# VectorE exponentials split with bitwise operations, and 512 more columns of channel 14 moved to VectorE in units 16 to 31

## What is computed

```python
def wl_step(acc, wl):
    cpm, iw = wl
    m = cpm[None, :, None, None]
    Qw = Q * m
    Kw = K * m
    scores = jnp.einsum('bhqd,bhkd->bhqk', Qw, Kw) * SCALE
    scores = scores * jnp.cos(KERR * scores * scores)
    attn = jax.nn.softmax(scores, axis=-1)
    out = jnp.einsum('bhqk,bhkd->bhqd', attn, V)
    return (acc + out * iw, None)
acc, _ = jax.lax.scan(wl_step, acc0, (cos_pm, interference_weights))
combined = acc / WL_CHANNELS
```

## Time and profile before

| | us |
|---|---|
| median of 3 runs | 3400.6 (3398.81 to 3402.12) |
| the profiled execution, its own time | 3405.69 |
| span of its trace | 3403.6 |
| ScalarE busy | 3316.2 (97%) |
| VectorE busy | 3240.6 (95%) |
| TensorE matmuls busy | 2650.6 (78%) |

### The profile page before, as it was taken

The page is one execution under the profiler, slowest core; times in us unless marked ns, Lnnn a source line. Parts: engine busy times, 40 slices in busy tenths (PEclk is TensorE's granted clock), DMA queues, the critical chain, the costliest instruction groups (busy, mean ns, idle before and its releaser), DMA issues.

```text
span 3403.6 us, 47606 instructions
## 1 busy us (share of the span) xinstructions
PE 2650.6 (78%) x20639; PEld 760.4 (22%) x20639; DVE 3240.6 (95%) x2747; ACT 3316.2 (97%) x611; POOL 229.2 (7%) x321
## 2 busy tenths in 40 slices
PE   7777877777777777778778788888877778788876
PEld 2212222222222222222222222222222222222224
DVE  7999999999999999999999999999999999999997
ACT  7999999999999999999999999999999999999992
POOL 0000000000000000000001111101111101111100
PEclk8999899999999999998999999899999999988888
DMA  1000000000000000000000000000000000000001
GB/s 49 1 1 1 1 1 1 1 1 1 1 1 1 1 1 1 1 15 1 1 1 3 4 3 4 2 1 4 2 4 2 4 1 2 4 3 16 2 17 31
DMA packets 21400, 16.05 MB, mean 5 GB/s; under 512 B 4865, under 2 KB 19602, under 8 KB 20946
## 3 DMA queue, kind: packets, MB, share of 16 engines
q1 hardware_dynamic: 19922, 12.28, 1.2%
q10 hardware_dynamic: 1152, 0.53, 0.1%
q0 software_dynamic: 128, 0.26, 0.0%
HBM read 7.70 MB, written 5.37 MB: 4 GB/s over the span
## 4 chain that ended last, share of the span: by engine, by line
ACT 59%; issue 32%; ACTq 4%; DVE 2%; PE 2%; DMA 0%; POOL 0%; DVEq 0%
ACT probs L694 56%; ACTq L684 4%; ACT probs L691 3%; PE psum L1392 1%; ACTq L688 0%; DVE s_t L921 0%; DVE probs L973 0%; DVE m_pad L909 0%; DMA iw<-nterference_weights_dram 0%; PE psum L948 0%; DVE probs L1003 0%; PE psum L1063 0%; PE psum L943 0%; PE psum L1106 0%; PE psum L933 0%
## 5 line engine op out<-in xcount | busy, mean ns | idle before, releaser
L694 ACT ACTIVATE probs<-s_t 128x8192 f32<-128x8192 f32 x447 | 3099.8, 7054 | 2.8 <-PE psum L1392 2.8
L1392 PE MATMUL psum<-probs,v_pad 128*27 128x512 f32 x15136 | 1909.2, 646 | 638.0 <-ACT probs L694 605.5
L1392 PEld LDWEIGHTS psum<-probs,v_pad 128*27 128x27 f32 x15136 | 462.1, 113 | 1996.9 <-issue 1022.1
L765 DVE SCALAR_TENSOR_TENSOR x_y<-s_t,c_last,x_2k 128x2048 f32<-128x2048 f32 (+1 forms) x160 | 369.6, 2310 | 2.3
L777 DVE SCALAR_TENSOR_TENSOR x_p<-x_p,x_y 128x2048 f32<-128x2048 f32 (+1 forms) x160 | 358.3, 2239 | 4.5
L785 DVE SCALAR_TENSOR_TENSOR x_p<-x_p,x_2k 128x2048 f32<-128x2048 f32 (+1 forms) x160 | 357.7, 2236 | 3.9
L781 DVE SCALAR_TENSOR_TENSOR x_p<-x_p 128x2048 f32<-128x2048 f32 (+1 forms) x160 | 357.3, 2233 | 2.4
L773 DVE SCALAR_TENSOR_TENSOR x_p<-x_y 128x2048 f32<-128x2048 f32 (+1 forms) x160 | 356.8, 2230 | 0.0
L921 DVE COPY s_t<-psum 128x2048 f32<-128x2048 f32 x128 | 292.2, 2284 | 9.4 <-PE psum L884 9.0
L909 DVE TENSOR_REDUCE m_pad<-psum 128x4 f32<-128x2048 f32 x128 | 292.4, 2286 | 5.8 <-PE psum L844 4.6
L762 DVE TENSOR_SCALAR x_2k<-s_t,c_last 128x2048 int16<-128x2048 f32 (+1 forms) x160 | 201.2, 1257 | 4.9 <-issue 1.0
(11 more groups left out here) (245 smaller groups left out, 1083.9 us busy)
## 6 DMA issues: line engine op xcount, KB each, us to landing
s_t<-in_L_attn_x_dram SPq DMA_DIRECT2D x4, 256.0 KB, 7.3
x_next_dram<-x_p SPq DMA_DIRECT2D x1, 1024.0 KB, 4.0
x_group<-x_next_dram SPq DMA_DIRECT2D x1, 1024.0 KB, 4.8
loop_memory<-in_L_attn_x_dram SPq DMA_DIRECT2D x8, 128.0 KB, 2.3
x_dram<-loop_memory SPq DMA_DIRECT2D x8, 128.0 KB, 1.8
out_dram<-loop_memory SPq DMA_DIRECT2D x8, 128.0 KB, 1.8
x_dram<-probs SPq DMA_DIRECT2D x2, 512.0 KB, 4.8
out_dram<-probs SPq DMA_DIRECT2D x2, 512.0 KB, 3.6
```

Of the source, the lines that this page charges most:

```text
L694: nc.scalar.activation(probs[:, (p + w) % 2, :], s_t[:, p, :], ACT.Exp, scale=scales[(p + w) % 2]).then_inc(s["exp_done"], 1)
L765: nc.vector.scalar_tensor_tensor(out=y, in0=scores, scalar=scale, in1=at, op0=ALU.mult, op1=ALU.subtract) \
L1392: last = nc.tensor.matmul(products_of(u, wg)[L * b:L * b + SLOTS * A, :], v_pad[:, p, b * T + kt, c0:c0 + SLOTS * A], probs[:, (p + w) % 2 ...
```

## The change

The split of a piece into integer and fraction is done in another way. Op 0 now writes an int32 fixed-point number with 23 fraction bits (the scale has a factor 2^23). Op 1 is a `tensor_scalar` of two bitwise operations that cuts the fraction bits out and sets the exponent of 1.0, in place of a `scalar_tensor_tensor` that read scores and integer. Op 2 is a `tensor_scalar` of two bitwise operations on int32 in place of arithmetic on int16. Ops 3 to 6 keep their form with other constants; op 6 reads an f32 power of two in place of a bf16 one. The work tile grows from 2 to 4 bytes an element, and `one_row` moves from a tile of its own, filled by GpSimd at the start, to a place in `s_t`, filled by VectorE in the last unit.

`SHARED_B` becomes (4, 4): in both groups ScalarE does 6144 columns of channel 14, and the fifth piece has all 2048 columns of its last key tile. In group 0 that is as before; in group 1 (units 16 to 31) 512 columns go from ScalarE to VectorE, and two matmul records from L1392 to L798. The tables for a sixth piece are written but `SHARED_B` leaves them unused: `pieces_of` is 5 for every unit, and the steps are those of before.

```diff
-SHARED_B = (0, 1)
-ACT_LAST = [T * X_COLS - (NB - b) * S for b in SHARED_B]
-PIECES = T + 1
+SHARED_B = (4, 4)
+ACT_LAST = [(T - 1) * X_COLS - (NB - b) * S for b in SHARED_B]
+def pieces_of(u):
+    return T + 1 + (SHARED_B[u // H] < NB)
+def piece_no(u, n):
+    return sum(pieces_of(v) for v in range(u)) + n
...
-        x_2k = sb("x_2k", [P, X_COLS], BF16)
-        x_n = x_2k[:].bitcast(I16)
+        x_i = sb("x_i", [P, X_COLS], I32)
...
-            w, start, cols = (W - 1, n * X_COLS, X_COLS) if n < T else (WA - 1, ACT_LAST[u // H], T * X_COLS - ACT_LAST[u // H])
+            w, start, cols = ((W - 1, n * X_COLS, X_COLS) if n < T else (WA - 1, (T - 1) * X_COLS, X_COLS) if n == T
+                              else (WA - 1, ACT_LAST[u // H], (T - 1) * X_COLS - ACT_LAST[u // H]))
...
-            at, y, t = x_n[:, 0:cols], x_y[:, 0:cols], x_p[:, piece % 2, 0:cols]
+            at, y, t = x_i[:, 0:cols], x_y[:, 0:cols], x_p[:, piece % 2, 0:cols]
             if op == 0:
                 dve.wait_ge(s["piece_ready"], piece + 1)
                 nc.vector.tensor_scalar(at, scores, scale, LOWEST_Y, ALU.mult, ALU.max).then_inc(s["piece_chain"], 1)
             if op == 1:
                 dve.wait_ge(s["piece_chain"], base + 1)
-                nc.vector.scalar_tensor_tensor(out=y, in0=scores, scalar=scale, in1=at, op0=ALU.mult, op1=ALU.subtract) \
+                nc.vector.tensor_scalar(y.bitcast(I32), at, FRACTION_BITS, ONE_BITS, ALU.bitwise_and, ALU.bitwise_or) \
                     .then_inc(s["piece_chain"], 1)
             if op == 2:
                 dve.wait_ge(s["piece_chain"], base + 2)
-                nc.vector.tensor_scalar(at, at, 127.0, 128.0, ALU.add, ALU.mult)
+                nc.vector.tensor_scalar(at, at, EXPONENT_TOP, EXPONENT_BITS, ALU.bitwise_xor, ALU.bitwise_and)
...
-                nc.vector.scalar_tensor_tensor(out=t, in0=t, scalar=EXP2_D, in1=x_2k[:, 0:cols], op0=ALU.add, op1=ALU.mult) \
+                nc.vector.scalar_tensor_tensor(out=t, in0=t, scalar=EXP2_D, in1=at.bitcast(F32), op0=ALU.add, op1=ALU.mult) \
                     .then_inc(s["piece_ready"], 1)
...
-                            for b in range(SHARED_B[g] if w == WA - 1 and kt == T - 1 else NB):
+                            for b in range(NB if w < WA - 1 or kt < T - 2 else SHARED_B[g] if kt == T - 2 else 0):
```

More of the change, by code:

```diff
@@ L73, in steps_of @@
 def steps_of(u, usual, last):
-    return last if u == UNITS - 1 else usual
+    return last if u == UNITS - 1 else usual[u // H]
 def due(u, w, usual, last):
@@ L218, in postln_kernel @@
         gate_b = scratch(G + EXPERTS)
+        one_row = scratch(P)
         assert taken[0] <= T * NB * S
@@ L227, in postln_kernel @@
         order = sb("order", [P, EXPERTS])
-        one_row = sb("one_row", [P, P])
         index = sb("index", [P, 3, MT], I32)
@@ L511, in _ @@
             nc.gpsimd.memset(quarter[:], 0.25)
-            nc.gpsimd.memset(one_row[:], 1.0)
             nc.gpsimd.memset(w_head[:], 0.0).then_inc(s["masks_zeroed"], 1)
@@ L784, in piece_dve @@
                 dve.wait_ge(s["piece_chain"], base + 5)
-                nc.vector.scalar_tensor_tensor(out=t, in0=t, scalar=EXP2_D, in1=x_2k[:, 0:cols], op0=ALU.add, op1=ALU.mult) \
+                nc.vector.scalar_tensor_tensor(out=t, in0=t, scalar=EXP2_D, in1=at.bitcast(F32), op0=ALU.add, op1=ALU.mult) \
                     .then_inc(s["piece_ready"], 1)
         def piece_pe(pe, n, u):
-            pe.wait_ge(s["piece_ready"], u * PIECES + (n + 2))
+            pe.wait_ge(s["piece_ready"], piece_no(u, n) + 2)
             if n == 0:
                 pe.wait_ge(s["o_copied"], max(u * NWG + 1, 2))
-            wg, kt = (NWG - 1, n) if n < T else (LAST_OF[WA - 1], T - 1)
+            wg, kt = (NWG - 1, n) if n < T else (LAST_OF[WA - 1], T - 1 if n == T else T - 2)
             c0 = VPAD if n < T else VPAD - A * SLOT_OF[WA - 1]
-            for b in range(NB) if n < T else range(SHARED_B[u // H], NB):
-                at = b * S if n < T else (b - SHARED_B[u // H]) * S
+            first, latest = SHARED_B[u // H] if n > T else 0, pieces_of(u) - 1
+            for b in range(first, NB):
+                at = (b - first) * S
                 last = nc.tensor.matmul(products_of(u, wg)[L * b:L * b + SLOTS * A, :],
-                                        v_pad[:, u % 2, b * T + kt, c0:c0 + SLOTS * A],
-                                        x_p[:, (u * PIECES + n) % 2, at:at + S], start=(n == 0), stop=(n == T - 1 or (n == T and u < UNITS - 1)))
+                                        v_pad[:, u % 2, b * T + kt, c0:c0 + SLOTS * A], x_p[:, piece_no(u, n) % 2, at:at + S],
+                                        start=(n == 0), stop=(n == T - 1 or (n >= T and n == latest and u < UNITS - 1)))
             last.then_inc(s["piece_used"], 1)
@@ L1132, in experts_memory_dve @@
             nc.vector.memset(zx, 0.0)
+            nc.vector.memset(one_row, 1.0)
         def experts_weights_dve(dve):
@@ L1378, in ff_step, with products_end_here @@
                             ff_pe(pe, stage, loop_chunk, k, ff_bank, comb_chunk)
+                    def products_end_here(u):
+                        return u == UNITS - 1 or pieces_of(u) > T + 1
                     for w in range(WA):
@@ L1395, in _ @@
                                     start=(kt == 0 and w in FIRST_OF),
-                                    stop=(w in LAST_OF and kt == (T - 2 if u == UNITS - 1 and w == WA - 1 and b >= SHARED_B[g] else T - 1)))
+                                    stop=(w in LAST_OF and kt == T - 1) or (w == WA - 1 and kt == T - 2 and products_end_here(u)))
                         last.then_inc(s["pv_done"], 1)
@@ L1494, in _ @@
                     dve.wait_ge(s["c2_step"], 7)
-                    nc.vector.tensor_scalar(c2_last[:], c2[:, WA - 1:W, :], LOG2_E, None, ALU.mult).then_inc(s["piece_used"], 1)
+                    nc.vector.tensor_scalar(c2_last[:], c2[:, WA - 1:W, :], LOG2_E * FRACTION, None, ALU.mult).then_inc(s["piece_used"], 1)
                 prep_dve(dve, step, 0, 0, first=True)
```

28 lines of the change are left out of this document (18 added, 10 removed).

## The result

The changed kernel takes 3408.12 us (median of 12 runs, 3404.13 to 3413.15) against 3402.87 us (12 runs of the kernel before in the same rounds, 3398.81 to 3406.43). The ratio is 1.0017, with a 95% interval of 1.0009 to 1.0025: about 6 us slower, between 3 and 8.5. The forecast was 3396.6 us and its range ended at 3404. The profiled execution took 3404.13 us of its own, with a span of 3402.2.

A forecast was written before the change was run, and what follows sets the result against it. The prediction took ScalarE to bound the kernel, with VectorE close behind. Its terms, -7.0 + 2 + 1 = -4.0 us, gave 3396.6 us, with a range of 3390 to 3404.

The forecast's parts named there:

- What bounds the kernel: Whole kernel: ScalarE, 97% busy and waiting only 2.8 us for TensorE, sets the pace of all 32 units.
- ScalarE's part: Channel 14, units 16 to 31: 512 columns fewer pace at 5.30 us against 5.74, 7.0 us saved in all.
- VectorE's part: VectorE's pieces: new ops 1 and 2 take 2440 ns in place of 3077, so VectorE still fits, just.
- GpSimd's longer chain: Behind group 1's statistics: four held GpSimd instructions grow 2.1 us, L1003 comes 1.8 us later, margins of 0.8 to 1.1 remain.
- I count two of the 8 even units with about 1 us: +2 us: Group 1, products behind L943: some run at the lower clock, so ScalarE waits in two even units, +2 us.
- in most pairs: Products of channels 1 and 2: GpSimd's delay reaches ScalarE, up to 16 us of waits, 3409.6 us; chance 0.18.
- +1 us for the product of channel 13: Group 1: channel 14's shorter exponential covers less of channel 13's product, so ScalarE sometimes waits for it, +1 us.
- The sum: Whole kernel: -7.0 + 2 + 1 = -4.0 us, giving 3396.6 us.

The follow-up runs named there:

- two operations earlier: Changed kernel with VectorE's piece operations of units 16 to 30 issued two earlier from step 10 on; 3396.93 us, ratio 0.9981 to the kernel before.
- one gap filled: Changed kernel with three idle matmuls on TensorE ahead of stage 3 in units 16 to 30; 3408.32 us, ratio 1.0011 to the kernel before.
- one operation earlier: Changed kernel with VectorE's piece operations of units 16 to 30 issued one earlier from step 10 on; 3397.12 us, ratio 0.9980 to the kernel before.
- operations in halves: Changed kernel with ops 3 to 6 of the fifth piece in units 16 to 31 each issued as two of 1024 columns; 3400.96 us, ratio 0.9991.

## Why the prediction was wrong

- **What bounds the kernel, and ScalarE's part.** Right. Channel 14 paces at 5.3 us, and where nothing else waits (two operations earlier) 6.5 of the 7.0 us arrive.
- **VectorE's part.** Right: 1284, 1244 and 1227 ns against 1284, 1220 and 1220. Op 1 lies 24 ns higher in the mean: in eight of the 160 pieces (one at 2617.75) it takes 1.64 us beside a GpSimd operation of 256 columns, elsewhere 1.16 to 1.30. A slip without effect: at 1284 ns an operation a unit's ten would take 0.64 us more, not 0.5. The old split with 2048 columns shows the other edge, 3437 us.
- **GpSimd's longer chain.** Right in mechanism and place: four operations of 2.2 to 2.3 us, a gap of 3.2 us for the 3.5 forecast (4.55 in three other units), L1022 waiting 1.73 us. From GpSimd's first operation to L1022 it is 10.84 us for 8.72, the 2.1 us of the forecast. But stage 3 comes 2.45 us later after channel 14, where I had 1.8: the chain starts 9.10 us after channel 14 for 8.78, and I had it 0.3 us earlier. What VectorE saves ahead of it goes into waits for TensorE, 0.32 us of it in the row at 2587.07. This alone would still have fitted in unit 24: at 3.64 us the product of channel 1 would have ended at 2617.82 + 3.64 = 2621.46, 0.7 us before ScalarE was ready for channel 3 (2601.29 + 20.88 = 2622.17). The Trainium skill ("SBUF — State Buffer", Who interferes with whom) calls the port pair that the two engines share an exclusive lock, and says that a VectorE instruction with two SBUF inputs contends with a GpSimd instruction that reads SBUF. The traces agree: GpSimd's operations are held for the length of VectorE's, 2.2 to 2.3 us beside whole ones and 1.1 us beside halves.
- **The step that failed** is "I count two of the 8 even units with about 1 us: +2 us". Six of eight did it, at 1.0 to 1.3 us: +6.3. I read the clock shares of whole units (0.95 to 0.98) as the chance that this product runs at full clock. But those shares are of the kernel before, with gaps of 0 or 1.7 us at this place (3.4 in unit 16), and the change makes just this gap longer. The trace of the kernel before already had a better rate: in units 16 to 31, of the 59 products with 2 to 3 us of idle TensorE just ahead of them 36 took over 3.8 us, of the 160 with less 23. It should have been sized per place: a gap of over 3 us ahead of nearly every such product, 6.4 us at worst for it, a margin of 0.8 to 1.1. The rival "in most pairs" was this case; I had it at 0.18, with 3409.6 us as its bound. That the measured time lies near this bound is partly luck, since 3.9 of the 10.2 us of waits come from another place.
- **A place that was left out.** I followed the delay to the products of channels 1 and 2 and stopped. VectorE, late behind the same chain, makes the row maxima late. TensorE stands 2.7 us for them, and the product of channel 4, slow in several units before as well, now ends after channel 6 is ready: +3.9 us. With one gap filled it was 7.8 of the 12.3 us that ScalarE waited.
- **+1 us for the product of channel 13.** In group 1 of the changed kernel no such wait came: 0. In group 0, where nothing was changed for ScalarE, such waits were 1.4 us (2.8 before), and between 0 and 2.8 us in the traces of the experiments that leave group 0 as it is: the +1 us was about what differs from one execution to the next.
- **The sum.** -7.0 + 6.3 + 3.9 = +3.2 us in place of -4.0; measured +5.3 between medians, interval +3 to +8.5, so some 2 us have no term. The profiled execution was the quickest of its twelve, with a tail (from channel 14 of unit 31 on) 4.8 us shorter than that of the profiled execution before; 2.9 us of this is its last product of channel 13, 3.64 us where it was 6.54. Read alone it would have hidden the loss.

## What to carry to other kernels

When an edit delays an instruction by more than the queue behind it has to spare, follow the delay to every engine that waits behind it, and price each matmul group behind a lengthened gap at the lower clock, by place and not by the unit's mean clock. Work moved onto an engine should not end up in the one stretch where others wait for its neighbour: moving one operation ahead of the statistics turned +6 us into -7, though the long wait that one sees in the profile (VectorE for GpSimd) grew. Saved time on an engine that hides behind another is worth nothing by itself and yet pays for the next move.

## What the hardware showed that I had not expected

- How long TensorE stands does not alone decide the clock. Behind 2.69 us ahead of stage 3 (one operation earlier) the product took 3.62 us, behind 2.0 us at the same place (operations in halves) 4.3 to 4.75 in five of six cases. Behind 2.68 us ahead of the scores it took from 3.64 to 6.35 us in one trace (one gap filled). Behind 3.1 to 4.6 us, six of seven products took 4.4 to 5.3 us and one 3.62. Why these differ was not settled.
- Idle matmuls in two gaps, which compute nothing, gave 7.3 us back between the medians, although at the end of unit 18 they made stage 3 0.9 us later.
- Bitwise `tensor_scalar` operations on int32 are as quick as the one on f32: 1227 and 1244 ns for 2048 columns (1284 for op 0, from f32) against 2289 for an operation on two tensors. The Trainium skill ("VectorE: DVE Perf Modes", The perf-mode tier table) gives 1227 ns for `tensor_scalar` on f32 and has no row for bitwise operations; in this trace they have the same time.
